# Normed x, context and rotated key: split in their own layout and turned by three DMA transposes per sequence instead of by TensorE

## The chip, the cores and the metric

The kernel runs on one core of a Trainium2 chip. The metric is the device time of one execution in microseconds (us). The core has a matrix engine (TensorE, PE in the profile, its weight loads PEld), VectorE (DVE), ScalarE (ACT), GpSimd (POOL) and SyncE (SP), whose instruction stream here does nothing but issue DMA transfers. Each engine works its own instruction list in order; they meet through semaphores (`wait_ge`, `then_inc`).

## What is computed

One transformer block over `x` (8 sequences of 128 tokens, width 256) and a context `ctx` of the same shape: layer norm, attention with 16 heads on 4 key/value groups over the 128 context tokens and 128 own tokens, output projection, residual; then a second layer norm, a shared feed-forward net and 8 experts of which each token takes 2.

```python
h = layernorm(x)
q, k, v = h @ wq, h @ wk, h @ wv                   # 16, 4, 4 heads of 128
q, k = rotate(rms_norm(q, qw)), rotate(rms_norm(k, kw))
k_ctx, v_ctx = rms_norm(ctx @ wk_ctx, kw), ctx @ wv_ctx
s = q @ concat(k_ctx, k).T / sqrt(128) + causal
x = x + (softmax(s) @ concat(v_ctx, v)) @ wo
x = x + moe(layernorm(x)) + shared(layernorm(x))
```

## The kernel before

Float32 values enter the matmuls as two fp16 parts, a high part (the rounded value) and a low part (value minus high part), and each product is three fp16 matmuls. ACT makes the high parts (L460, a helper `copy`), DVE most of the low parts (L908, a helper `low`); in the profile these lines stand for many tiles, so groups are told apart by the tile's name.

The attention part is a pipeline over the sequences b = 0 to 7 with four steps g = 0 to 3 each, one for each key/value group (4 heads). Each engine has a function `row(b, first, last)` with the same steps: written out for b = 0, as a loop for b = 1 to 6, written out for b = 7. In step g PE does: `scores(b, g)` (L1282, L1304), the turning of the rotated queries one step ahead (`q_turn`, L1261), the turning of the previous step's probabilities (`turn_probs`, L1315), the query projection two steps ahead (`q`, L1172), and `mix` of the previous step (probabilities times values, L1325). In between stand, in step 0, the value projections; in step 1, `out_proj(b - 1)`, 48 matmuls (L1352), and then `turn_inputs(b + 1)`; in step 2, after `q(b + 1, 0)`, the projections `kc(b + 1)` and `k(b + 1)` of context key and key; in step 3, `kc_turn` and `k_turn(b + 1)`. So the inputs and keys of sequence b + 1 are made within the row of b.

Three things are turned for each next sequence nb = b + 1 (contraction needs the width on the partitions):

- normed x: ACT makes `x_hi` and POOL `x_lo` in step 1, `turn_inputs` (L1197) turns both on PE into the PSUM bank `turn`, ACT's `in_copies` copies them to `xT`. Its first reader is `q(nb, 0)` in step 2.
- context: `ctx_b` is turned in float32 (L1200) into the same bank; ACT makes `cT_hi` from it, DVE `cT_lo` (`cT_low`, after `residual(b - 1)`, which waits for `out_proj`). First reader: `kc(nb)`.
- rotated key: POOL's `k_scale` (L758) writes `k_rot` in step 2, `k_turn` (L1229) turns it in step 3 into `proj[0]`, ACT's `k_copy` and DVE's `k_low` make `kT_hi` and `kT_lo`, both between other work of step 3. First reader: `scores(nb, 0)`.

ACT's step 3 runs `q_copy(nb, 0)`, `p_copy`, then `exps(b, 3)` (four exponentials, L549) with `kc_copy` and `k_copy` between the second and third. POOL ends step 2 with `k_roots`, `k_scale` and `q_roots(nb, 0)` and begins step 3 with `q_add(nb, 1)`. SP has little to do in the rows: one load of `ctx_b` each (L413, after `in_turned`) and, for the weights of the experts, three loads and six DMA transposes (L419, L424) between rows. After the attention it issues 16 DMA transposes (L447) of 128x1024 bf16 (256 KB), one for each expert and token half.

PE's clock has two levels; `keep_warm` in the opening runs matmuls for nothing to hold the upper one.

Of the kernel before, what the change touches and what calls it, by code (L numbers as in the profile page):

```python
# [5 lines left out]
ALU = mybir.AluOpType  # L6
# [38 lines left out]
def xattn_moe_kernel(nc, x, ctx, wq, wk, wv, wo, wk_ctx, wv_ctx, q_norm_w, k_norm_w,  # L45
# [14 lines left out]
    with ExitStack() as stack:  # L60
# [57 lines left out]
        x_hi = sb("x_hi", [P, D], FP16)  # L118
        x_lo = sb("x_lo", [P, D], FP16)
        xT = sb("xT", [P, 2, DC, P], FP16)  # L120
        cT = sb("cT", [P, DC, P])
        cT_hi = sb("cT_hi", [P, DC, P], FP16)
        cT_lo = sb("cT_lo", [P, DC, P], FP16)
# [27 lines left out]
        kT_hi = sb("kT_hi", [P, G, 2, P], FP16)  # L151
        kT_lo = sb("kT_lo", [P, G, 2, P], FP16)
# [101 lines left out]
        in_turned = sem("in_turned")  # L254
        xT_ready = sem("xT_ready")
        cT_high = sem("cT_high")
# [20 lines left out]
        k_high = sem("k_high")  # L277
        k_ready = sem("k_ready")
# [102 lines left out]
        def _(sp):  # L381
# [29 lines left out]
            def next_ctx(b):  # L411
                sp.wait_ge(in_turned, b)
                sp.dma_start(ctx_b[:], ctx[b, :, :]).then_inc(d_ctx, 16)  # L413

# [12 lines left out]
            next_ctx(2)  # L427
            next_ctx(3)
            sp.wait_ge(w1_cast, 4)
            sp.dma_start(w1_32[:], w3.rearrange("e h d -> h e d")).then_inc(d_w3, 16)  # L430
            turn_up(w1T, w1_b)
            next_ctx(4)
            sp.wait_ge(w3_cast, 4)
            sp.dma_start(w1_32[:].rearrange("p e (c h) -> p (e c) h", c=DC),
                         w2.rearrange("e (c p) h -> p (e c) h", p=P)).then_inc(d_w2, 16)
            turn_up(w3T, w3_b)
            next_ctx(5)
            sp.wait_ge(w2_cast, 4)
            turn_down()
            with sp.Fori(6, B) as b:  # L440
                next_ctx(b)
# [16 lines left out]
        def _(act):  # L458
# [10 lines left out]
            def ln_high(nb):  # L469
                act.wait_ge(ln_xs, nb + 1)  # L470
                seen(act, in_turned, nb)
                copy(x_hi[:], xs[:]).then_inc(ln_hi, 1)

            def in_copies(nb):
                act.wait_ge(in_turned, nb + 1)
                copy(xT[:].rearrange("p a c t -> p (a c t)"), turn[:, 0:256].bitcast(FP16)).then_inc(xT_ready, 1)
                if isinstance(nb, int) and nb == 0:
                    copy(flat(cT[:]), turn[:, 256:512], CW).then_inc(cT_ready, 1)
                else:
                    copy(flat(cT_hi[:]), turn[:, 256:512], C_SCALE).then_inc(cT_high, 1)  # L480
# [20 lines left out]
            def k_squares(nb):  # L501
                seen(act, k_mean, nb)
                squares(proj[1], k_ss, k_junk, k_t12, nb + 1, float(P) ** -0.5, k_sq)
# [22 lines left out]
            def k_copy(nb):  # L526
                act.wait_ge(k_turned, nb + 1)
                copy(kT_hi[:, :, 1, :], proj[0][:].rearrange("p (g t) -> p g t", g=G), K_SCALE).then_inc(k_high, 1)
# [74 lines left out]
            def row(b, first, last):  # L603
                for g in range(G):
# [7 lines left out]
                    exps(b, g, (kc_copy, k_copy) if g == 3 and not last else ())  # L612
# [8 lines left out]
                    if g == 1 and not last:  # L621
                        in_copies(b + 1)
# [12 lines left out]
                    if g == 0:  # L635
                        vc_copy(b)
                    if first and g == 1:
# [58 lines left out]
        def _(pool):  # L696
# [6 lines left out]
            nc.gpsimd.memset(eps_k[:], RMS_EPS * XW ** 2)  # L703
# [33 lines left out]
            def ln_low(nb):  # L737
                pool.wait_ge(ln_hi, nb + 1)
                seen(pool, in_turned, nb)
                nc.gpsimd.tensor_tensor(x_lo[:], xs[:], x_hi[:], ALU.subtract).then_inc(ln_lo, 1)  # L740
# [13 lines left out]
            def k_scale(nb):  # L754
                pool.wait_ge(k_added, nb + 1)
                pool.wait_ge(k_root, nb + 1)
                seen(pool, k_turned, nb)
# [117 lines left out]
        def _(dve):  # L875
# [35 lines left out]
            def cT_low(nb):  # L911
                dve.wait_ge(cT_high, nb)
# [660 lines left out]
```

## Time and profile before

| | us |
|---|---|
| median of 3 runs | 366.74 |
| lowest, highest | 364.2, 368.2 |
| profiled execution, its own time | 366.01 |
| its span | 364.3 |
| busy: PE, DVE, ACT, POOL | 329.9, 316.9, 263.7, 166.5 |

The profile is of one execution. Its span is 1.7 us shorter than that execution's own time. The prologue takes some 30 us, the eight rows run from there to about 310 us, the feed-forward part fills the rest. In the timeline each line gives start, duration, engine, line, operation, output<-inputs, shapes and count; in square brackets stands how long the engine was idle before it and what ended that. A duration of a PE matmul includes its way through the array, so the distance between two starts, not the duration, is what a matmul takes of PE.

### The profile page before, as it was taken

What the parts mean: (1) busy time and instruction counts of PE and PEld (TensorE: products, weight loads), DVE (VectorE), ACT (ScalarE), POOL (GpSimd) and SP (SyncE); (2) the same over time, 40 slices, a digit from 0 to 9 for tenths busy, and PEclk for the clock granted to TensorE, in tenths of its full rate; (3) what the DMA queues carried; (4) which work ended last, traced back from release to release, by engine and by line L of the source; (5) the groups of instructions that cost most, each with busy time, mean ns of one, the idle gap of its engine ahead of it and who ended that gap; (6) DMA issues with size and microseconds to landing.
All of it is one profiled execution on the core that took longest, in us unless ns stands there. A gap on an engine that the chain in (4) does not pass through costs nothing.

```text
span 364.3 us, 7426 instructions
## 1 busy us (share of the span) xinstructions
PE 329.9 (91%) x2296; PEld 223.4 (61%) x2296; DVE 316.9 (87%) x602; ACT 263.7 (72%) x916; POOL 166.5 (46%) x241
## 2 busy tenths in 40 slices
PE   6788698799999999999999999999999999987894
PEld 6365455376667666866576657565856687754351
DVE  1779999998999899989999998999899987967643
ACT  3668989576986798679768976897599748447341
POOL 4467656652755175427532734263426230362600
PEclk9899989999999999999999999999999999999999
DMA  6977000000042005200300000000000000167844
GB/s 177 380 238 230 18 0 2 1 2 14 1 126 47 14 0 128 45 14 3 58 6 8 0 0 14 0 0 0 0 0 0 3 0 0 23 123 75 159 75 129
DMA packets 34835, 19.25 MB, mean 53 GB/s; under 512 B 24056, under 2 KB 32256, under 8 KB 34816
## 3 DMA queue, kind: packets, MB, share of 16 engines
q1 hardware_dynamic: 34816, 19.02, 20.6%
q8 instruction: 9, 0.15, 0.2%
q14 instruction: 10, 0.08, 0.1%
HBM read 12.20 MB, written 1.05 MB: 36 GB/s over the span
## 4 chain that ended last, share of the span: by engine, by line
PE 35%; DVE 24%; ACT 18%; issue 10%; POOL 6%; DMA 3%; SPq 1%; DVEq 1%; ACTq 0%; POOLq 0%
PE proj L1352 10%; ACT probs L549 7%; DVE probs L982 5%; PE pt_ps L1315 5%; PE turn L1261 3%; DVE nmax L970 3%; POOL q_rot L772 3%; PE o_ps L1325 3%; DVE pT_lo L908 3%; PE proj L1172 3%; PE sc_ps L1282 3%; ACT pT_hi L460 2%; DVE q_t L899 2%; ACT kc_junk L493 2%; DMA wq<-in_L_xattn_wq_dram 2%
## 5 line engine op out<-in xcount | busy, mean ns | idle before, releaser
L549 ACT ACTIVATE probs<-sc_ps,nbias,q_r 128x256 f32<-128x256 f32 x128 | 70.8, 573 | 2.8 <-DVE nbias L974 2.8
L772 POOL TENSOR_TENSOR q_rot<-q_t 128x512 f32<-128x512 f32 x32 | 42.4, 1325 | 41.3 <-DVE q_t L901 40.5
L982 DVE TENSOR_SCALAR probs<-probs,rden 128x256 f32<-128x256 f32 x128 | 51.2, 461 | 1.1
L460 ACT ACTIVATE pT_hi<-pt_ps 128x512 f16<-128x512 f32 x64 | 34.8, 597 | 10.1 <-PE pt_ps L1315 10.1
L493 ACT ACTIVATE q_junk<-proj 128x128 bf16<-128x128 f32 x128 | 34.0, 294 | 10.8 <-DVE q_t L901 10.8
L1172 PE MATMUL proj<-wq_hi,xT 128*128 128x512 f16 x128 | 39.2, 389 | 2.1 <-DVE wq_lo L892 2.1
L908 DVE SCALAR_TENSOR_TENSOR pT_lo<-pt_ps,pT_hi 128x512 f16<-128x512 f32 x64 | 40.9, 680 | 0.1
L970 DVE TENSOR_REDUCE nmax<-sc_ps 128x4 f32<-128x1024 f32 x32 | 38.8, 1214 | 1.5 <-PE sc_ps L1304 1.5
L729 POOL TENSOR_TENSOR q_r<-q_me,power 128x4 f32<-128x4 f32 x32 | 33.4, 1044 | 2.5
L460 ACT ACTIVATE qT_hi<-turn 128x512 f16<-128x512 f32 x32 | 19.5, 610 | 20.5 <-PE turn L1261 20.5
L1315 PE MATMUL pt_ps<-ident,probs 128*128 128x128 f32 x256 | 34.1, 277 | 0.2
L1352 PE MATMUL proj<-wo_hi,oT_hi 128*128 128x256 f16 x112 | 30.5, 273 | 0.0
L1352 PE MATMUL proj<-wo_lo,oT_hi 128*128 128x256 f16 x112 | 30.5, 273 | 0.0
L1352 PE MATMUL proj<-wo_hi,oT_lo 128*128 128x256 f16 x112 | 30.5, 273 | 0.0
L1315 PEld LDWEIGHTS pt_ps<-ident,probs 128*128 128x128 f32 x256 | 29.4, 143 | 0.6 <-DVE probs L982 0.3
L1261 PE MATMUL turn<-ident,q_rot 128*128 128x128 f32 x128 | 19.8, 278 | 10.9 <-POOL q_rot L772 5.3
L493 ACT ACTIVATION_READ_ACCUMULATOR q_junk<-proj 128x1 f32 x128 | 28.5, 226 | 0.0
L549 ACT ACTIVATION_READ_ACCUMULATOR probs<-sc_ps,nbias,q_r 128x1 f32 x128 | 27.5, 215 | 0.0
L1325 PE MATMUL o_ps<-pT_hi,v_hi 128*128 128x512 f16 x64 | 24.3, 379 | 2.8 <-DVE pT_lo L908 2.8
L908 DVE SCALAR_TENSOR_TENSOR oT_lo<-o_ps,oT_hi 128x512 f16<-128x512 f32 x32 | 21.9, 685 | 5.4 <-ACT oT_hi L460 5.4
L460 ACT ACTIVATE oT_hi<-o_ps 128x512 f16<-128x512 f32 x32 | 19.6, 613 | 7.8 <-PE o_ps L1325 7.8
L1282 PE MATMUL sc_ps<-kT_hi,qT_hi 128*128 128x256 f16 x128 | 24.5, 273 | 0.5 <-ACT probs L549 0.2
(221 smaller groups left out, 882.8 us busy)
## 6 DMA issues: line engine op xcount, KB each, us to landing
wq<-in_L_xattn_wq_dram SPq DMA_DIRECT2D x4, 512.0 KB, 8.4
w<-in_L_ffn_w_dram SPq DMA_DIRECT2D x2, 1024.0 KB, 9.9
wq<-in_L_xattn_wo_dram SPq DMA_DIRECT2D x1, 2048.0 KB, 8.2
ctx_b<-in_ctx_dram SPq DMA_DIRECT2D x8, 128.0 KB, 2.0
out_dram<-x_all SPq DMA_DIRECT2D x4, 256.0 KB, 2.2
x_all<-in_x_dram SPq DMA_DIRECT2D x1, 896.0 KB, 12.0
wkc<-in_L_xattn_wk_ctx_dram SPq DMA_DIRECT2D x1, 512.0 KB, 3.9
wk<-in_L_xattn_wk_dram SPq DMA_DIRECT2D x1, 512.0 KB, 4.9
```

The lines of the kernel that those rows point to most:

```text
L460: return nc.scalar.activation(out_, in_, ACT.Copy, scale=scale)
L493: last = nc.scalar.activation(junk[:, head], bank[:, head], ACT.Square, scale=scale, accum_out=dst[:, h:h + 1])
L549: last = nc.scalar.activation(probs[:, h, :], sc_ps[:, h, :], ACT.Exp, bias=nbias[:, h:h + 1], scale=q_r[:, g, h:h + 1], accum_out=den[:, ...
L772: nc.gpsimd.tensor_tensor(q_rot[:], q_t1[:], q_t2[:], ALU.add).then_inc(q_added, 1)
L908: return nc.vector.scalar_tensor_tensor(out=lo, in0=src, scalar=scale, in1=hi, op0=ALU.mult, op1=ALU.subtract)
L970: nc.vector.tensor_reduce(nmax[:], sc_ps[:], AX_X, ALU.max, negate=True).then_inc(s_max, 1)
L982: last = nc.vector.tensor_scalar(probs[:, h, :], probs[:, h, :], rden[:, h:h + 1], None, ALU.mult)
L1172: last = nc.tensor.matmul(bank[:], xT[:, a, c, :], w[:, c, cols], start=(n == 0), stop=(n == 3 * DC - 1))
L1282: nc.tensor.matmul(sc_ps[:, h, :], a[:, h * P:(h + 1) * P], w[:, g, :, :].rearrange("p a t -> p (a t)"), start=start, stop=False, skip_gro ...
L1315: last = nc.tensor.transpose(pt_ps[:, a, h * P:(h + 1) * P], probs[:, h, a * P:(a + 1) * P], ident[:])
L1325: last = nc.tensor.matmul(o_ps[:], v[:, a, g * P:(g + 1) * P], p[:, a, :], start=(a == 0 and i == 0), stop=(a == 1 and i == 2))
L1352: last = nc.tensor.matmul(proj[0][:, 0:D], o[:, h // R, (h % R) * P:(h % R + 1) * P], w[:, h, :], start=(h == 0 and i == 0), stop=(h == H ...
```

## The change

TensorE no longer turns x, context and key for nb >= 1 (for nb = 0 all stays). Instead:

- Context: ACT's new `ctx_high` splits `ctx_b` as it lies, at the end of step 0 of the row before; DVE's `ctx_low` takes the place of `cT_low` in step 1. Both halves lie in the memory of `cT` (`c16`), and a DMA transpose writes `cT16`.
- x: `x_hi` and `x_lo` lie side by side (`x16`), and a DMA transpose writes `xT`.
- Key: ACT's `k_round` takes the rounding of `k_rot` ahead of `exps(b, 3)`, POOL's `k_rest` the low part at the head of its step 3, both into `k16` (the memory of `k_t1`), and a DMA transpose of 256 KB writes the halves of `kT`. `k_turn`, `k_copy` and `k_low` go for nb >= 1. The scale 2^4 moves into `eps_k` and the squares.
- SP issues them in a fixed order for each row: context, load of the next context, x, key; the weights' transfers come after the key of their row. The waits are in the diff. On PE, `q(nb, 0)` and `k(nb)` wait for `d_xT`, `kc(nb)` for `d_cT`, `scores(nb, 0)` for `d_kT`.

The core of the diff, in the order of the file: SP, then ACT (`ctx_high`, `k_round`), POOL (`k_rest`), DVE (`ctx_low`), and last PE (`k_turn` and `turn_inputs` go from its row).

```diff
+            for b in range(B - 1):
+                nb = b + 1
+                sp.wait_ge(c_high, nb)
+                sp.wait_ge(c_low16, nb)
+                sp.wait_ge(vc_proj, nb)
+                sp.dma_start_transpose(cT16[:].rearrange("p s c t -> p (s c) t"),
+                                       c16.rearrange("p s d -> p (s d)")).then_inc(d_cT, 16)
+                if nb + 1 < B:
+                    sp.dma_start(ctx_b[:], ctx[nb + 1, :, :]).then_inc(d_ctx, 16)
+                sp.wait_ge(ln_hi, nb + 1)
+                sp.wait_ge(ln_lo, nb + 1)
+                sp.wait_ge(q_proj, G * nb)
+                sp.wait_ge(v_proj, nb)
+                sp.dma_start_transpose(xT[:].rearrange("p s c t -> p (s c) t"),
+                                       x16[:].rearrange("p s d -> p (s d)")).then_inc(d_xT, 16)
+                sp.wait_ge(k_high16, nb)
+                sp.wait_ge(k_low16, nb)
+                sp.wait_ge(s_done, G * nb)
+                sp.dma_start_transpose(kT[:, :, :, 1, :].rearrange("p s g t -> p (s g) t"),
+                                       k16.rearrange("p s n -> p (s n)")).then_inc(d_kT, 16)
...
+            def ctx_high(nb):
+                act.wait_ge(d_ctx, 16 * (nb + 1))
+                act.wait_ge(vc_proj, nb)
+                seen(act, d_cT, 16 * (nb - 1))
+                copy(c16[:, 0], ctx_b[:], C_SCALE).then_inc(c_high, 1)
+            def k_round(nb):
+                act.wait_ge(k_norm, nb + 1)
+                copy(k16[:, 0], k_rot[:]).then_inc(k_high16, 1)
...
-                    exps(b, g, (kc_copy, k_copy) if g == 3 and not last else ())
+                    if g == 3 and not last:
+                        k_round(b + 1)
+                    exps(b, g, (kc_copy,) if g == 3 and not last else ())
...
-                    if g == 1 and not last:
-                        in_copies(b + 1)
...
+            def k_rest(nb):
+                pool.wait_ge(k_high16, nb)
+                nc.gpsimd.tensor_tensor(k16[:, 1], k_rot[:], k16[:, 0], ALU.subtract).then_inc(k_low16, 1)
...
+                    if g == 3 and not last:
+                        k_rest(b + 1)
...
+            def ctx_low(nb):
+                dve.wait_ge(c_high, nb)
+                low(c16[:, 1], ctx_b[:], C_SCALE, c16[:, 0]).then_inc(c_low16, 1)
...
-                        k_low(b + 1)
...
-                        cT_low(b + 1)
+                        ctx_low(b + 1)
...
-                        k_turn(b + 1)
...
-                        if not last:
-                            turn_inputs(b + 1)
```

The orders below are the compiled lists of instructions. First POOL, from the end of step 2 into step 3 of a row, before: `k_r` and `k_rot` are the key's factor and its scaling, `q_me` and `q_r` are `q_roots(nb, 0)`, `q_rot` is `q_add(nb, 1)`.

```order
L729 TENSOR_TENSOR k_r<-k_me,power 128x4 [waits k_mean]
L758 TENSOR_TENSOR k_rot<-k_sum,k_r 128x512 [waits k_turned,k_root,k_added]
L727 TENSOR_TENSOR q_me<-q_ss,eps_q 128x4 [waits q_sq,s_exp]
L729 TENSOR_TENSOR q_r<-q_me,power 128x4 [waits q_mean]
L772 TENSOR_TENSOR q_rot<-q_t 128x512 [waits q_turned,q_t12]
```

The same place of the changed kernel:

```order
L762 TENSOR_TENSOR k_r<-k_me,power 128x4 [waits k_mean]
L797 TENSOR_TENSOR k_rot<-k_sum,k_r 128x512 [waits k_high16,k_root,k_added]
L760 TENSOR_TENSOR q_me<-q_ss,eps_q 128x4 [waits q_sq,s_exp]
L762 TENSOR_TENSOR q_r<-q_me,power 128x4 [waits q_mean]
L803 TENSOR_TENSOR k_t<-k_rot,k_t 128x512 [waits k_high16]
L815 TENSOR_TENSOR q_rot<-q_t 128x512 [waits q_turned,q_t12]
```

The key's low part (L803) stands behind the two operations of `q_roots(nb, 0)` and ahead of `q_add(nb, 1)`. Next ACT in step 3 before: `p_copy` (pT_hi), then `exps(b, 3)` with the two key copies within.

```order
L460 ACTIVATE pT_hi<-pt_ps 128x512 [waits p_turned]
L460 ACTIVATE pT_hi<-pt_ps 128x512
L549 ACTIVATE probs,den<-sc_ps,nbias,q_r 128x256 [waits p_turned,s_bias]
L549 ACTIVATE probs,den<-sc_ps,nbias,q_r 128x256
L460 ACTIVATE kT_hi<-turn,kw_scaled 128x4x128 [waits kc_turned]
L460 ACTIVATE kT_hi<-proj 128x4x128 [waits k_turned]
L549 ACTIVATE probs,den<-sc_ps,nbias,q_r 128x256 x2
```

The same place of the changed kernel:

```order
L481 ACTIVATE pT_hi<-pt_ps 128x512 [waits p_turned]
L481 ACTIVATE pT_hi<-pt_ps 128x512
L481 ACTIVATE k_t<-k_rot 128x512 [waits k_norm]
L580 ACTIVATE probs,den<-sc_ps,nbias,q_r 128x256 [waits p_turned,s_bias]
L580 ACTIVATE probs,den<-sc_ps,nbias,q_r 128x256
L481 ACTIVATE kT<-turn,kw_scaled 128x4x128 [waits kc_turned]
L580 ACTIVATE probs,den<-sc_ps,nbias,q_r 128x256 x2
```

The copy out of `proj` within the exponentials is gone, and a rounding of `k_rot` (L481, into `k_t`) with a wait for `k_norm` stands ahead of all four. Last SP in two rows of the changed kernel (before there was one `ctx_b` load a row):

```order
L436 DMA_TRANSPOSE cT<-cT 128x4x128 [waits vc_proj,c_low16,c_high]
L439 DMA ctx_b<-in_ctx_dram 128x256
L444 DMA_TRANSPOSE xT<-x 128x4x128 [waits q_proj,v_proj,ln_lo,ln_hi]
L449 DMA_TRANSPOSE kT<-k_t 128x8x128 [waits s_done,k_low16,k_high16]
L453 DMA w_32<-in_L_ffn_w_dram 128x8x256 [waits w1_cast]
L423 DMA_TRANSPOSE w1T<-w_b 128x8x128 x2
```

The transpose of x stands behind the transpose of the context and behind the load of the next context.

## Rows read from the trace of the kernel before

**Rows 1.** The page: busy time of each engine, share of the span, count
```profile
PE 329.9 (91%) x2296; PEld 223.4 (61%) x2296; DVE 316.9 (87%) x602; ACT 263.7 (72%) x916; POOL 166.5 (46%) x241
```

**Rows 2.** Stretch, its length, busy PE, PEld, DVE, ACT, POOL, granted clock
```profile
189.80:225.30 35.50, 34.24 (x248) 23.75 (x246) 33.84 (x68) 28.32 (x108) 15.77 (x23) 1.00 0.01 4
```

**Rows 3.** Timeline from the end of out_proj to the next query projection
```profile
189.00 0.27 PE L1352 MATMUL proj<-wo_hi,oT_lo 128*128 128x256 f16 x1
189.11 0.28 PE L1197 MATMUL turn<-ident,x_hi 128*128 128x128 f16 x2
...
189.34 0.39 PE L1200 MATMUL turn<-ident,ctx_b 128*128 128x128 f32 x2
...
189.91 0.36 SPq L413 DMA_DIRECT2D ctx_b<-in_ctx_dram  x1
...
190.66 0.42 DVE L908 SCALAR_TENSOR_TENSOR cT_lo<-turn,cT_hi 128x256 f16<-128x256 f32 x1
```

**Rows 4.** Timeline of PE, step 2 and 3 of the same row
```profile
192.83 1.04 PE L1315 MATMUL pt_ps<-ident,probs 128*128 128x128 f32 x8
193.71 0.59 PE L1172 MATMUL proj<-wq_hi,xT 128*128 128x512 f16 x2
...
195.00 1.03 PE L1185 MATMUL turn<-wk,cT_hi 128*128 128x512 f16 x4
...
204.62 0.66 PE L1229 MATMUL proj<-ident,k_rot 128*128 128x128 f32 x4 [0.31 <-POOL k_rot L758]
206.40 0.38 PE L1282 MATMUL sc_ps<-kT_hi,qT_hi 128*128 128x256 f16 x2
...
216.76 0.63 PE L1261 MATMUL turn<-ident,q_rot 128*128 128x128 f32 x4 [0.41 <-DVE v_lo L908]
```

**Rows 5.** DMA issues: tile, kind, count, KB each, median us from issue to landing
```profile
ctx_b<-in_ctx_dram SPq DMA_DIRECT2D x8, 128.0 KB, 2.0
out_dram<-x_all SPq DMA_DIRECT2D x4, 256.0 KB, 2.2
w2T<-w_b SPq DMA_TRANSPOSE x2, 3.2
```

**Rows 6.** Timeline of SP's queue: two transposes of 256 KB each
```profile
175.08 2.61 SPq L424 DMA_TRANSPOSE w2T<-w_b  x2
```

**Rows 7.** Timeline of POOL and ACT around the key in step 3
```profile
203.52 1.04 POOL L758 TENSOR_TENSOR k_rot<-k_sum,k_r 128x512 f32<-128x512 f32 x1
...
204.79 1.01 POOL L729 TENSOR_TENSOR q_r<-q_me,power 128x4 f32<-128x4 f32 x1
...
203.58 0.57 ACT L549 ACTIVATE probs<-sc_ps,nbias,q_r 128x256 f32<-128x256 f32 x1
```

**Rows 8.** Timeline of ACT and POOL: the split of x
```profile
221.43 0.44 ACT L460 ACTIVATE x_hi<-xs 128x256 f16<-128x256 f32 x1
221.95 0.67 POOL L740 TENSOR_TENSOR x_lo<-xs,x_hi 128x256 f16<-128x256 f32 x1 [4.58 <-ACT x_hi L460]
```

**Rows 9.** Timeline of PE in the row of sequence 0 and after it
```profile
29.05 0.66 PE L1261 MATMUL turn<-ident,q_rot 128*128 128x128 f32 x4 [1.96 <-POOL q_rot L772]
...
45.28 1.85 PE L1315 MATMUL pt_ps<-ident,probs 128*128 128x128 f32 x8
46.91 1.06 PE L1172 MATMUL proj<-wq_hi,xT 128*128 128x512 f16 x2
...
49.12 1.03 PE L1185 MATMUL turn<-wk,cT_hi 128*128 128x512 f16 x4
...
60.82 0.38 PE L1282 MATMUL sc_ps<-kT_hi,qT_hi 128*128 128x256 f16 x2
...
69.78 0.39 PE L1325 MATMUL o_ps<-pT_hi,v_hi 128*128 128x512 f16 x1 [2.52 <-DVE pT_lo L908]
```

**Rows 10.** Busy time by stretch, as rows 2; the granted clock follows POOL
```profile
42.30:44.80 2.50, 0.00 (x0) 0.02 (x1) 2.50 (x7) 2.50 (x5) 2.42 (x3) 1.00 0.00 0
44.80:48.80 4.00, 3.99 (x17) 2.81 (x18) 3.97 (x5) 2.72 (x7) 2.99 (x1) 0.57 0.00 0
```

More of the change, by code:

```diff
@@ L277, in xattn_moe_kernel @@
         k_high = sem("k_high")
+        k_high16 = sem("k_high16")
+        k_low16 = sem("k_low16")
         k_ready = sem("k_ready")
@@ L470, in ln_high @@
                 act.wait_ge(ln_xs, nb + 1)
-                seen(act, in_turned, nb)
-                copy(x_hi[:], xs[:]).then_inc(ln_hi, 1)
+                if isinstance(nb, int) and nb == 1:
+                    act.wait_ge(in_turned, 1)
+                elif not isinstance(nb, int) or nb:
+                    act.wait_ge(d_xT, 16 * (nb - 1))
+                copy(x_hi, xs[:]).then_inc(ln_hi, 1)
             def in_copies(nb):
@@ L636, in row @@
                         vc_copy(b)
+                    if g == 0 and not last:
+                        ctx_high(b + 1)
                     if first and g == 1:
@@ L738, in ln_low @@
                 pool.wait_ge(ln_hi, nb + 1)
-                seen(pool, in_turned, nb)
-                nc.gpsimd.tensor_tensor(x_lo[:], xs[:], x_hi[:], ALU.subtract).then_inc(ln_lo, 1)
+                if isinstance(nb, int) and nb == 1:
+                    pool.wait_ge(in_turned, 1)
+                elif not isinstance(nb, int) or nb:
+                    pool.wait_ge(d_xT, 16 * (nb - 1))
+                nc.gpsimd.tensor_tensor(x_lo, xs[:], x_hi, ALU.subtract).then_inc(ln_lo, 1)
             def l2_root(b):
@@ L756, in k_scale @@
                 pool.wait_ge(k_root, nb + 1)
-                seen(pool, k_turned, nb)
+                if isinstance(nb, int) and nb == 1:
+                    pool.wait_ge(k_turned, 1)
+                elif not isinstance(nb, int) or nb:
+                    pool.wait_ge(k_high16, nb - 1)
                 nc.gpsimd.tensor_tensor(k_rot[:].rearrange("p (g d) -> p g d", g=G),
@@ L1204, in kc @@
             def kc(nb):
-                pe.wait_ge(cT_ready, nb + 1)
-                seen(pe, q_ready, G * nb)
-                if not (isinstance(nb, int) and nb == 0):
+                if isinstance(nb, int) and nb == 0:
+                    pe.wait_ge(cT_ready, 1)
+                else:
+                    pe.wait_ge(d_cT, 16 * nb)
+                    pe.wait_ge(q_ready, G * nb)
                     pe.wait_ge(wc_low, 1)
@@ L1239, in q @@
                 if g == 2:
-                    pe.wait_ge(k_ready, b + 1)
+                    if isinstance(b, int) and b == 0:
+                        pe.wait_ge(k_ready, 1)
+                    pe.wait_ge(q_sq, G * b + 1)
                 if g == 3:
@@ L1254, in q_turn @@
                     pe.wait_ge(v_ready, b + 1)
-                if g == 3 and last:
+                if g == 3:
                     pe.wait_ge(q_ready, G * b + g)
-                if g == 3 and not last:
-                    pe.wait_ge(xT_ready, b + 2)
-                    pe.wait_ge(cT_ready, b + 2)
                 for h in range(R):
@@ L1287, in scores @@
                 if g == 0:
-                    pe.wait_ge(k_high, b + 1)
+                    if isinstance(b, int) and b == 0:
+                        pe.wait_ge(k_high, 1)
+                    else:
+                        pe.wait_ge(d_kT, 16 * b)
                     pe.wait_ge(kc_high, b + 1)
@@ L1399, in _ @@
             keep_warm(32)
-            turn_inputs(0)
+            turn_inputs()
             keep_warm(16)
@@ L1412, in _ @@
             keep_warm(16)
-            k_turn(0)
+            k_turn()
             keep_warm(8)
```

95 lines of the change are left out of this document (48 added, 47 removed).

## Prediction

> **What bounds the kernel now.** I read the page first [rows 1]: PE is busy 91% of the span, VectorE 87%, so a reader might think that every matmul taken from PE pays. Then the busy time of one loop row [rows 2]: it takes 35.50 us and PE is busy 34.24 of it, VectorE 33.84. The eight rows are a chain in which PE runs from one operation to the next almost without a gap, and what decides is at which points PE would have to wait for something from outside. Two such points matter here: the first reader of the new x, `q(nb, 0)` at 193.71, and the first reader of the new key, `scores(nb, 0)` at 206.40 [rows 4]. The row shown is that of one b in the loop; all times below are in its clock.
>
> **What goes from PE.** `turn_inputs` begins right behind out_proj at 189.11, and its last two transposes start at 189.34 [rows 3]: with them some 0.45 us of PE. `k_turn` takes four transposes at 204.62 and 0.31 us of waiting ahead [rows 4], some 0.75 us. ACT loses three copies and gains two, VectorE loses one operation. All of this can only come back where nothing later is waited for.
>
> **Step A, x.** In the new order of SP the context is turned first. Its low part, `ctx_low`, stands on VectorE where `cT_low` stands now, behind the residual of out_proj: 190.66 + 0.42 = 191.08 [rows 3]; the shape is the same, so I keep that. SP started its load 0.18 us after the turning ended (189.34 + 0.39 = 189.73, start 189.91) [rows 3], so the context's transpose starts at 191.25. SP was held 2.61 us by two transposes of 256 KB [rows 6], 1.3 each; half of that for 128 KB, 0.65 (an estimate from that row), gives 191.9. The load of the next context holds SP 0.36 [rows 3], so the transpose of x starts at about 192.35. How long 128 KB take to land turned, no row shows. From below: a plain load of 128 KB lands in 2.0; from above: a transpose of 256 KB lands in 3.2 [rows 5]. I take 2.6, the middle, as half the data should save about half of what separates them. x lands at 194.95 and `q(nb, 0)` starts at 195.0 and not at 193.71: **1.3 us later** (0.7 to 1.9). PE, 0.45 early without `turn_inputs`, stands 1.75 us. The context, issued 1.1 us ahead, is there before `kc(nb)`, which stood at 195.00 and now comes at 196.3.
>
> **Step B, the key.** The projections, squares and factors that make `k_rot` follow `q(nb, 0)` in one chain, so `k_rot`, finished at 203.52 + 1.04 = 204.56 [rows 7], comes 1.3 later, at 205.85 (0.5 at least, since ACT's exponentials stand in that chain too). Then, new in line: ACT's `k_round`; `x_hi` took 0.44 for half the shape [rows 8], so 0.6 to 0.65: 206.5. It stands ahead of `exps(b, 3)`, which began at 203.58 [rows 7] and now begins at 206.5. `k_rest` on POOL can't start then, because the order shows the two operations of `q_roots(nb, 0)` between `k_rot` and it; they end at 204.79 + 1.01 = 205.80 now [rows 7], 1.24 behind `k_rot`, so 207.1. `k_rest` takes twice the 0.67 of `x_lo` [rows 8], 1.3: 208.4. SP 0.2: 208.6. A transpose of 256 KB lands in 3.2 [rows 5]: 211.8, and `scores(nb, 0)` starts at 211.9 instead of 206.40: **5.5 us later**, step A's 1.3 included. The last work ahead of it, `mix(b, 2)`, is over at about 207, so PE stands near 5 us. In that shadow lies the removed `k_turn`, which therefore returns nothing; the same holds for `turn_inputs` in that of step A. Nobody but PE waits for the key, but everything is behind PE: the next maximum, exponentials and probabilities all start from these scores. The exponentials of (b, 3), three microseconds late, end at about 209.3 and are thus covered; were the key there in time, they would be the next thing late.
>
> **What is caught up.** From `scores(nb, 0)` to the end of the next out_proj PE had one wait worth naming, 0.41 for `v_lo` [rows 4]. VectorE and ACT can use the stall to be ready, PE can't be faster: 0.4 us back. Leaves 5.1 us a row.
>
> **Step C, the clock.** In the row of sequence 0 PE stood idle from 42.30 to 44.80, and behind it the granted clock was 0.57 on average over 4 us, that is mostly the lower level of 1.2 GHz [rows 10]. The eight transposes of `turn_probs` then took 46.91 - 45.28 = 1.63 us and six projection matmuls 49.12 - 46.91 = 2.21 [rows 9]; the same in the loop row took 193.71 - 192.83 = 0.88 and 195.00 - 193.71 = 1.29 [rows 4]: 1.67 us lost for one fall. An idle of 1.96 us ahead of 29.05 left the matmuls behind it as they were (0.66 for the group against 0.63) [rows 9, 4]. So I expect the 5 us of step B to bring a fall and the 1.75 us of step A none. Part of the low stretch lies in the stall itself, so 1.5 us a fall. The Trainium skill, TensorE: Matmul & The Clock Gate, section "The HAM clock gate", has the same two levels and the drop after idleness; here the trace agrees, with the 2.5 us above.
>
> **Sum.** A loop row gets 5.1 + 1.5 = 6.6 us longer; six of them (b = 1 to 6): 39.6. The row of b = 0 prepares sequence 1 in the same way: its scores, at 60.82 [rows 9], come about 5.5 later, but PE waited 2.52 us at 69.78 for `pT_lo` [rows 9], which can take up as much; with the clock 5.5 - 2.5 + 1.5 = 4.5. The row of b = 7 prepares nothing: 0. The weights' transposes follow the key of their row, some 15 us ahead of the next context: 0. Together 44.1 on the profiled execution's 366.01, which is 0.7 below the median of the runs: **410 us**.
>
> A rule that speaks otherwise: the Trainium skill, Advanced Engine Details and Errata, section "X-Bar Transpose (TRN2)", says that transpose DMAs are as fast as regular ones. The rows differ for 256 KB: 3.2 turned, 2.2 plain [rows 5]. By the rule it would be rival 3 below.
>
> **The rivals.**
> 1. The clock stays up in the stalls of step B. For it: 1.96 us of idle did not lower it [rows 9]; against it: 2.5 us did [rows 10], and here it is 5. 366 + 6 x 5.1 + 3 = 400 us.
> 2. The stall of step A also lowers the clock, or the transposes land late (two more transfers share the queue): 1.5 a row more, 7 x 1.5 = 10.5: 421 us.
> 3. A turned transfer costs what a plain one does, 2.0 for 128 KB and 2.2 for 256 KB [rows 5]: 0.6 less in step A, 1.0 less in step B, seven times: 11 less, 399 us.
> 4. The other side: the transfers are hidden and PE gets its 0.45 and 0.75 us back each time: 7 x 1.2 = 8.4, 358 us. This decides itself where the key is turned within the time between `k_rot` at 204.56 and `scores(nb, 0)` at 206.40, 1.84 us; rounding, low part and transfer would have to fit, and the transfer alone takes 3.2.
>
> **Chances and range.** Forecast 0.60; rival 1 0.13; rival 2 0.15; rival 3 0.09; rival 4 0.01; a stall of step B nearly covered by something that I read wrongly, with less than 1% lost, 0.02. The range reaches from the bounds of rivals 1 and 3, less 0.8 a row if the key's chain moves by 0.5 only (399 - 6 = 393), to rival 2 with x landing at 3.2 (421 + 4 = 425). A measurement of this kernel tells about 1% from no change. Faster by over 1% 0.01, within 1% 0.02, slower 0.97.
>
> **What would show it.** In the changed kernel's waits: PE's `q` and `scores` lines wait for DMA `xT` and `kT`, seven times each, about 1.7 and 5 us. The loop row is 42 us long instead of 35.5. The granted clock falls to the lower level behind each wait for `kT`, not behind that for `xT`. The landing of `kT` is 3.2 and `xT` 2.6. POOL's L803 starts right behind `q_r`, and `probs` of step 3 starts behind `k_t<-k_rot`. Wrong would be: a row under 38 us, a key transfer issued before 207 of this clock, or a wait for something else at `scores`.

## The result, and the profile after

The changed kernel took 415.31 us (median of 4, 414.71 to 416.41), the kernel before 365.82 on the same chip (364.2 to 368.2): a ratio of 1.134, 95% interval 1.129 to 1.138. The forecast was 410, with a range of 393 to 425. The two profiled executions have spans of 414.0 and 364.3 us, 49.7 apart.

The page of the changed kernel: busy time by engine as in [rows 1], the granted clock in tenths by fortieths of the span, and two groups of matmuls (busy time, mean ns of one, idle time of PE ahead of them and what ended it).

```profile
PE 339.2 (82%) x2222; PEld 226.8 (55%) x2226; DVE 313.1 (76%) x595; ACT 260.6 (63%) x909; POOL 175.4 (42%) x248
...
PEclk9899897999899898999699989988999899999998
...
L1335 PE MATMUL sc_ps<-kT,qT_hi 128*128 128x256 f16 x256 | 56.3, 303 | 32.6 <-DMA kT<-k_t 32.6
...
L1218 PE MATMUL proj<-wq_hi,xT 128*128 128x512 f16 x128 | 40.0, 395 | 21.1 <-DMA xT<-x 18.7
```

The change takes ten transposes from PE in each of seven rows, 70 in all: its weight loads fall by just that, its matmuls by 74, as a few records of matmuls are missing. PE is nevertheless busy 9.3 us longer than in [rows 1], since more of its matmuls run at the lower clock. And it stands still for 32.6 us ahead of the scores and 18.7 us ahead of the projection of x, both times for a transposed transfer. Those two waits come to 51.3 us, beside 49.7 us of longer span. Not all of it is new: 5.0 us of the x wait stand in the row of sequence 0, ahead of 49.73, where the kernel before waited 2.56 us for VectorE's `cT_lo`. The x wait is 2.3 to 2.6 us in the loop rows of b = 1 to 5 and 1.63 in that of b = 6, which has no next context to load.

When the eight residuals on VectorE ran (first and last start; the first belongs to sequence 0, the last ends the row that prepares nothing), of before and then of after:

```profile
L992 DVE SCALAR_TENSOR_TENSOR x_all<-proj,x_all x8: 423/425/425, 82.8 to 317.8; 128x256 f32 x6, 128x256 f32<-128x256 f32 x2
```
```profile
L1039 DVE SCALAR_TENSOR_TENSOR x_all<-proj,x_all x8: 424/425/425, 88.2 to 367.5; 128x256 f32 x6, 128x256 f32<-128x256 f32 x2
```

By the first one the changed kernel is 5.4 us behind, and between the first and the last another (367.5 - 88.2) - (317.8 - 82.8) = 44.3 are lost: 7.4 in each of six loop rows. Behind the last nothing is lost or won: 367.5 - 317.8 is the whole 49.7.

One loop row of the changed kernel, x and context first (the timeline; what stands in brackets is idle time ahead and what ended it):

```profile
217.81 0.42 DVE L1039 SCALAR_TENSOR_TENSOR x_all<-proj,x_all 128x256 f32 x1 [0.23 <-PE proj L1409]
...
218.97 0.39 DVE L953 SCALAR_TENSOR_TENSOR cT<-ctx_b,cT 128x256 f16<-128x256 f32 x1
...
219.43 1.19 SPq L436 DMA_TRANSPOSE cT<-cT  x1
...
220.66 0.58 SPq L439 DMA_DIRECT2D ctx_b<-in_ctx_dram  x1
...
221.41 1.19 SPq L444 DMA_TRANSPOSE xT<-x  x1
...
224.19 0.59 PE L1218 MATMUL proj<-wq_hi,xT 128*128 128x512 f16 x2 [2.39 <-DMA xT<-x]
```

The low part of the context (`cT_lo` in [rows 3]) serves as the common mark. From it to `q(nb, 0)` it was 193.71 - 190.66 = 3.05 us in [rows 3, 4]; now it is 224.19 - 218.97 = 5.22, so x comes 2.2 us late. SP, the engine that issues the transfers, is occupied ("held" from here on) 1.19 us by the context's transpose and 0.58 by the next context's load before x gets its turn.

Then the key, in the same row and view:

```profile
233.83 1.04 POOL L797 TENSOR_TENSOR k_rot<-k_sum,k_r 128x512 f32<-128x512 f32 x1
...
234.91 0.63 ACT L481 ACTIVATE k_t<-k_rot 128x512 f16<-128x512 f32 x1 [1.00 <-POOL k_rot L797]
235.11 1.01 POOL L762 TENSOR_TENSOR q_r<-q_me,power 128x4 f32<-128x4 f32 x1
235.43 0.38 PE L1382 MATMUL o_ps<-pT_lo,v_hi 128*128 128x512 f16 x1
235.44 0.55 ACT L580 ACTIVATE probs<-sc_ps,nbias,q_r 128x256 f32<-128x256 f32 x1
...
236.09 1.15 POOL L803 TENSOR_TENSOR k_t<-k_rot,k_t 128x512 f16<-128x512 f32 x1
...
237.32 1.24 SPq L449 DMA_TRANSPOSE kT<-k_t  x1
...
240.62 0.58 PE L1335 MATMUL sc_ps<-kT,qT_hi 128*128 128x256 f16 x2 [4.80 <-DMA kT<-k_t]
```

`k_rot` is ready at 234.87; rounding, two small operations of POOL that are no part of the key (one of them L762), the low part and the transfer follow one after the other, and PE is idle from 235.81 on. From the mark to these scores it is 21.65 us, against 206.40 - 190.66 = 15.74 in [rows 3, 4]: 5.9 us late.

The clock around the two stalls (busy time by stretch, columns as in [rows 2], the granted clock ahead of the last two), first the key's stall in this row, then the x stall of the next:

```profile
239.00:240.00 1.00, 0.00 (x0) 0.00 (x0) 0.83 (x4) 0.82 (x4) 0.45 (x2) 1.00 0.87 162
240.00:241.00 1.00, 0.39 (x3) 0.29 (x4) 0.55 (x1) 0.00 (x0) 0.83 (x1) 0.72 0.00 0
241.00:242.00 1.00, 1.00 (x6) 0.73 (x5) 0.00 (x0) 0.00 (x0) 0.00 (x0) 0.50 0.00 0
...
243.00:244.00 1.00, 1.00 (x9) 0.87 (x7) 0.20 (x1) 0.00 (x0) 0.00 (x0) 0.57 0.00 0
...
268.00:269.00 1.00, 1.00 (x3) 0.30 (x2) 0.59 (x1) 0.00 (x0) 0.00 (x0) 0.50 0.00 0
...
270.00:271.00 1.00, 1.00 (x4) 0.32 (x3) 0.96 (x4) 0.00 (x0) 0.00 (x0) 0.50 0.00 0
```

The clock is at its lower level, 0.50 or 1.2 GHz, for some 3.4 us at the end of the key's stall and behind it (from 240.4 to 243.9). Behind the x stall in the row shown above it stayed at 1.00; in the next row, and in one other of the six, it fell as well. In all there are ten low stretches between 45 and 330 us, where the kernel before has one: seven at the key, three at x (the third is in the row of sequence 0, where the kernel before has its own). Two of the seven at the key, from 66.3 and from 196.0, are 6.8 us long.

### The profile page after: what moved, and what is told of

The parts are those of the page before. It is cut to its first block and busy times, and to the rows that moved or that the text cites. A ratio compares the mean times of both kernels' runs of the same rounds, so it can differ in the third digit from the quotient of the medians.

```text
span 414.0 us, 7308 instructions
## 1 busy us (share of the span) xinstructions
PE 339.2 (82%) x2222; PEld 226.8 (55%) x2226; DVE 313.1 (76%) x595; ACT 260.6 (63%) x909; POOL 175.4 (42%) x248
## 5 line engine op out<-in xcount | busy, mean ns | idle before, releaser
L1335 PE MATMUL sc_ps<-kT,qT_hi 128*128 128x256 f16 x256 | 56.3, 303 | 32.6 <-DMA kT<-k_t 32.6
L1218 PE MATMUL proj<-wq_hi,xT 128*128 128x512 f16 x128 | 40.0, 395 | 21.1 <-DMA xT<-x 18.7
L1335 PEld LDWEIGHTS sc_ps<-kT,qT_hi 128*128 128x128 f16 x256 | 26.7, 107 | 46.1 <-issue 35.8
L481 ACT ACTIVATE qT_hi<-turn 128x512 f16<-128x512 f32 x32 | 19.6, 611 | 44.6 <-PE turn L1314 44.6
L481 ACT ACTIVATE pT_hi<-pt_ps 128x512 f16<-128x512 f32 x64 | 34.8, 598 | 10.4 <-PE pt_ps L1372 9.8
L1372 PE MATMUL pt_ps<-ident,probs 128*128 128x128 f32 x256 | 35.0, 282 | 0.4 <-DVE probs L1029 0.3
L762 POOL TENSOR_TENSOR q_r<-q_me,power 128x4 f32<-128x4 f32 x32 | 33.5, 1046 | 2.5
L481 ACT ACTIVATE oT_hi<-o_ps 128x512 f16<-128x512 f32 x32 | 19.4, 607 | 22.9 <-PE o_ps L1382 22.9
L1372 PEld LDWEIGHTS pt_ps<-ident,probs 128*128 128x128 f32 x256 | 30.6, 147 | 0.9 <-DVE probs L1029 0.9
L944 DVE TENSOR_TENSOR q_t<-proj,q_cos 128x512 f32<-128x512 f32 x32 | 21.8, 683 | 11.6 <-PE proj L1218 11.6
L1218 PEld LDWEIGHTS proj<-wq_hi,xT 128*128 128x128 f16 x128 | 12.4, 101 | 31.6 <-issue 16.0
L1335 PE MATMUL sc_ps<-kT,qT_lo 128*128 128x256 f16 x128 | 28.0, 305 | 0.1
```

The lines of the kernel that those rows point to most:

```text
L481: return nc.scalar.activation(out_, in_, ACT.Copy, scale=scale)
L762: nc.gpsimd.tensor_tensor(r, me, power[:], ALU.pow).then_inc(root, 1)
L1218: last = nc.tensor.matmul(bank[:], xT[:, a, c, :], w[:, c, cols], start=(n == 0), stop=(n == 3 * DC - 1))
L1335: nc.tensor.matmul(sc_ps[:, h, :], a[:, h * P:(h + 1) * P], w[:, g, :, :].rearrange("p a t -> p (a t)"), start=start, stop=False, skip_gro ...
L1372: last = nc.tensor.transpose(pt_ps[:, a, h * P:(h + 1) * P], probs[:, h, a * P:(a + 1) * P], ident[:])
```

## The experiments

Each was timed beside the kernel before, which had medians of 366.95, 367.04 and 366.92 us in the three groups that ran together; the changed kernel's own 415.31 is compared by ratio.

**1. x ahead of the context on SP.** The rest of the changed kernel stays.

```diff
+                sp.wait_ge(ln_hi, nb + 1)
...
+                sp.dma_start_transpose(xT[:].rearrange("p s c t -> p (s c) t"),
+                                       x16[:].rearrange("p s d -> p (s d)")).then_inc(d_xT, 16)
                 sp.wait_ge(c_high, nb)
...
                     sp.dma_start(ctx_b[:], ctx[nb + 1, :, :]).then_inc(d_ctx, 16)
-                sp.wait_ge(ln_hi, nb + 1)
...
-                sp.dma_start_transpose(xT[:].rearrange("p s c t -> p (s c) t"),
-                                       x16[:].rearrange("p s d -> p (s d)")).then_inc(d_xT, 16)
```

> The changed kernel with one edit: SP issues the transpose of x ahead of that of the context and of the context load. Its waits are the same; x is split some 4 us before the context's low part is there. Theory (x is late only because it stands in SP's queue behind the context, and the whole chain from the query projection to the rotated key follows it): PE's wait for xT (2.4 to 2.7 us a row in the changed kernel) goes to zero, the key's transpose is issued about 2 us earlier in the row, so a row gets 2.1 us shorter plus the occasional fall of the clock behind the wait for x: 415 - 7 x 2.5 = about 398 us. Rival (the late x only fills time that the key's transfer would leave idle anyway): PE's wait for kT grows by what that for xT loses, the time stays at 413 to 415.

Measured: 399.16 us, ratio 1.089 (1.084 to 1.095), 16 us less than the changed kernel from the order of two entries alone. The waits of PE between 85 and 330 us (sum, times, longest):

```profile
PE sc_ps L1335 <- DMA kT<-k_t: 27.7, 6, 4.7
PE turn L1314 <- POOL q_rot L815: 3.3, 6, 0.5
```

The wait for x is gone and that for the key has kept its length. So the stall ahead of `q(nb, 0)` came from SP's order. The transfer itself takes 2.4 us to land instead of 2.5, but it now starts while PE still has other work. The clock's part is mixed into these 16 us: no low stretch is left at x, while those at the key are now 6.8 us long in six of the seven rows, with 4.7 to 5.5 us of each behind the stall's end.

**2 and 3. The key turned by PE again,** once with the order of the change (2) and once with x first (3). `k_turn` on PE, `k_copy` on ACT and `k_low` on VectorE are back as in the kernel before.

```diff
-                sp.dma_start_transpose(kT[:, :, :, 1, :].rearrange("p s g t -> p (s g) t"),
-                                       k16.rearrange("p s n -> p (s n)")).then_inc(d_kT, 16)
...
-                    if g == 3 and not last:
-                        k_round(b + 1)
-                    exps(b, g, (kc_copy,) if g == 3 and not last else ())
+                    exps(b, g, (kc_copy, k_copy) if g == 3 and not last else ())
...
-                        k_rest(b + 1)
...
+                        k_turn(b + 1)
```

> The changed kernel with the key turned by TensorE again for every sequence (k_turn, k_copy, k_low as before; k_round, k_rest and the key's DMA transpose gone), x and context still by DMA in the changed kernel's order. Theory (two separate costs, some 2.1 us a row from x and some 5.5 from key and clock): the row is 35.5 + 2.1 - 0.4 = 37 to 38 us, and the clock falls in some rows behind the wait for x: 366 + 7 x 2 + up to 4 = 380 to 384 us. Rival (nearly all of the cost hangs on the key): 366 to 370 us, with the wait for xT absorbed by later slack.

> Both edits together: key by TensorE as before, x and context by DMA with x issued first. Nothing waits for a transfer any more if the theory holds: x lands during the output projection, the context (issued at 191.25 of the row shown of the kernel before, landing in 2.5) at 193.8, ahead of its reader at 194.5. What is left is the pure gain of turn_inputs leaving TensorE: 0.45 us in each of 7 rows, 366 - 3 = 363 us. Rival (the row is set by VectorE and ACT as much as by PE, so that 0.45 us of PE are worth nothing): 366 us. Second rival (the context becomes the late one): a wait for cT at kc of 0.3 to 1 us a row, 366 to 370 us.

Measured: 383.61 us, ratio 1.047 (1.041 to 1.053), and 366.41 us, ratio 0.998 (0.996 to 1.001). In (2) PE's wait for x is what it was (13.4 us in six rows). In (3) no wait for a DMA is left in the loop rows, which are 35.1 us long (x's transposes start at 190.84 and 225.93), 0.4 less than in [rows 2]: that is all of the removed PE work that ever comes back. It isn't seen in the total, because the row of sequence 0 loses about as much; experiment 4 shows how much. The timeline of (3) there:

```profile
46.77 1.20 SPq L442 DMA_TRANSPOSE cT<-cT  x1
...
47.08 0.59 PE L1201 MATMUL proj<-wq_hi,xT 128*128 128x512 f16 x2
...
50.10 0.68 DVE L937 SCALAR_TENSOR_TENSOR qT_lo<-turn,qT_hi 128x512 f16<-128x512 f32 x1
50.88 2.72 PE L1214 MATMUL turn<-wk,cT 128*128 128x512 f16 x6 [3.21 <-issue]
```

PE stands 3.2 us ahead of `kc`, the first reader of the context, and the granted clock is 0.50 behind it. At first sight the context is late, and the expectation of experiment 4 takes it so. But the context's transposes land at most 2.5 us after their issue in this trace, this one by 49.3. `kc` also waits for VectorE's `qT_lo` (`q_ready`), and that ends at 50.78, 0.1 us ahead of PE's start. The profile names no releaser; by these times it is `qT_lo`.

**4. The low part of the context earlier in (3),** so that its transpose doesn't wait.

```diff
                     if g == 3 and not last:
                         kc_low(b + 1)
...
+                    if g == 1 and not last:
+                        ctx_low(b + 1)
...
-                    if g == 1 and not last:
-                        ctx_low(b + 1)
```

(The two places are in VectorE's program; the first is its earlier one within a step.)

> Key by TensorE as before, x and context by DMA with x issued first, and VectorE's low part of the context moved from behind the residual to ahead of the normalisation of the same step, 3 to 4 us earlier. Without that move the loop rows took 35.1 us instead of 35.5, but in the row of sequence 0 TensorE waited for the context and the clock fell behind it, and the time was that of the kernel before. Theory (with the context early too, no transfer is waited for anywhere and 0.4 us a row stay): 366.9 - 7 x 0.4 = 364 us, no wait for cT. Rival (the move only makes VectorE's probabilities 0.4 us later in each row and gives the gain back): 367 us.

Measured: 365.85 us, ratio 0.996 (0.993 to 0.999), between the theory's 364 and the rival's 367. The context's first transpose now starts at 41.06 instead of 46.77 and has landed by 43.6, and yet:

```profile
47.59 0.68 DVE L937 SCALAR_TENSOR_TENSOR qT_lo<-turn,qT_hi 128x512 f16<-128x512 f32 x1
...
48.37 2.72 PE L1214 MATMUL turn<-wk,cT 128*128 128x512 f16 x6 [2.87 <-issue]
...
71.19 0.39 PE L1359 MATMUL o_ps<-pT_hi,v_hi 128*128 128x512 f16 x1 [3.50 <-DVE pT_lo L937]
```

PE still stands 2.87 us ahead of `kc`, again up to 0.1 us behind the end of `qT_lo`. So the wait in this row is VectorE's, not the transfer's. The residuals of this kernel, first and last start:

```profile
L1021 DVE SCALAR_TENSOR_TENSOR x_all<-proj,x_all x8: 409/425/425, 85.3 to 317.8; 128x256 f32 x6, 128x256 f32<-128x256 f32 x2
```

Before it was 82.8 and 317.8. The six loop rows gain 2.5 us, 0.4 each, and the row of sequence 0 loses the same 2.5. Its second stall, for `pT_lo`, is 3.50 us where it was 2.52 [rows 9], and the clock falls behind it, where it stayed up before. This is the only version whose interval lies below the kernel before, and by under half a per cent: x and context by DMA gain next to nothing even when neither is waited for.

**5. The key alone turned by DMA,** x and context by PE as in the kernel before.

```diff
+                sp.dma_start_transpose(kT[:, :, :, 1, :].rearrange("p s g t -> p (s g) t"),
+                                       k16.rearrange("p s n -> p (s n)")).then_inc(d_kT, 16)
...
+                    if g == 3 and not last:
+                        k_round(b + 1)
...
+                        k_rest(b + 1)
...
-                        k_turn(b + 1)
```

> Only the key is turned by DMA; x and the context are turned by PE as in the kernel before. Theory (the two stalls add up): the key's chain starts 2.1 us earlier than in the changed kernel, so scores are about 3.7 us late instead of 5.8, and the clock still falls behind them in every row (1.6). 3.7 + 1.6 - 0.4 of catching up = 4.9 in each of six loop rows, about 3 in the row of sequence 0: 366 + 32 = 398; it should also be what is left of 415.3 when the 17.6 us of x and context (the run with the key on PE, 383.6 against 366) are taken off. Rival (the x stall costs nothing of its own once the key stall is there, because the key transfer is what everything waits for): 408 to 415. Loop rows about 40.4 us, PE's wait at the scores about 3.5 us.

Measured: 400.44 us, ratio 1.091 (1.084 to 1.098): near the first theory's 398 and well below the rival's 408. The key alone costs 9.1%, x and context alone (2) 4.7%: together 13.8%, beside 13.4% for the whole change. In the total the two stalls add. The row in this kernel:

```profile
142.29 1.23 SPq L438 DMA_TRANSPOSE kT<-k_t  x1
...
145.81 0.61 PE L1310 MATMUL sc_ps<-kT,qT_hi 128*128 128x256 f16 x2 [4.92 <-DMA kT<-k_t]
```

PE stands 4.6 to 4.9 us in the six loop rows here too, not the 3.5 that I had expected. The load of the next context, at 125.03 in this row and at 189.91 in [rows 3], is the common mark: the scores come 20.78 us behind it instead of 16.49, so 4.3 late. I had taken them for 3.7 late; the removed `k_turn` lies in the shadow besides.

**6. Idle matmuls that keep the clock up.** The changed kernel, with matmuls whose result nobody reads ahead of the two waits: 24 ahead of x and 56 ahead of the key.

```diff
+            def hold_clock(count):
+                for _ in range(count):
+                    nc.tensor.matmul(proj[0][:, 0:P], identb[:], causal[:], start=True, stop=True)
...
-                    normed(b)
...
+                    if not isinstance(b, int) or b:
+                        hold_clock(24)
+                    normed(b)
...
+                        pe.wait_ge(q_sq, G * b + 1)
+                        pe.wait_ge(q_t12, G * b + 1)
+                        hold_clock(56)
                         pe.wait_ge(d_kT, 16 * b)
```

> The changed kernel with TensorE kept busy in its two stalls by matmuls whose result nobody reads: 24 of 128 columns ahead of the wait for xT, 56 ahead of the wait for kT (about 0.06 us each, 1.4 and 3.4 us, both less than the waits). They change nothing but the clock. Theory (each fall to 1.2 GHz costs some 1.6 us, 7 falls behind kT and some 3 behind xT): the granted clock stays at 1.00 in the rows and the time falls by 7 x 1.6 + 3 x 1.7 = 16 to about 399 us, with waits for the transfers as long as before. Rival (the low clock only slows matmuls that other engines would make wait anyway): clock at 1.00 and still 412 to 415 us.

(The wait for x, `normed(b)`, is also moved behind two other waits, so that it comes last.) Measured: 398.51 us, ratio 1.088 (1.082 to 1.094), the 399 of the theory. The clock line of its page:

```profile
PEclk9899989999999999999999999999999999999998
```

Behind the sixth fortieth of the span the clock stays up all through the rows. The transfers are as late as before: from the first query projection to the scores it is 16.41 us in a row of this kernel (214.87 to 231.28) and 16.43 in the row shown of the changed one (224.19 to 240.62). So the 16.8 us less than 415.31 are the price of the clock alone, and the 398.51 - 366.95 = 31.6 us that remain are that of lateness.

**7. The same, ahead of x only.**

```diff
-                    normed(b)
...
+                    if not isinstance(b, int) or b:
+                        hold_clock(24)
+                    normed(b)
```

> As the changed kernel, with 24 additional matmuls of 128x128 ahead of PE's wait for x, whose result nobody reads; none ahead of the wait for the key. They keep PE busy in the x stall. Theory (the clock also falls behind the x stall, in the row of sequence 0 and in two of six loop rows as the changed kernel's trace shows, 1.6 us each): 415.3 - 5 = 410. Rival (no fall behind x costs anything, since each is hidden by the key stall later in the row): 414 to 416. The granted clock stays at 1.00 behind every wait for x and is at 0.50 behind every wait for the key.

Measured: 411.7 us, ratio 1.121 (1.114 to 1.128), between the two theories' 410 and 414 to 416; its interval ends 0.001 below where that of the changed kernel begins. By this the clock behind x would cost about 4 us of the 16.8. Behind the x stall of the six loop rows it stayed up, as meant; in the row of sequence 0, where PE still stood 3.63 us, it fell. I don't take this one number for more: in this execution two of four low stretches at the key between 120 and 320 us were 6 to 7 us long, in the changed kernel's one of four, so that part of what x gave back may have been lost again there.

**8. The key in two transfers of 128 KB,** the high half as soon as ACT has rounded it.

```diff
-                sp.wait_ge(k_high16, nb)
-                sp.wait_ge(k_low16, nb)
-                sp.dma_start_transpose(kT[:, :, :, 1, :].rearrange("p s g t -> p (s g) t"),
-                                       k16.rearrange("p s n -> p (s n)")).then_inc(d_kT, 16)
+                sp.wait_ge(k_high16, nb)
+                sp.dma_start_transpose(kT[:, 0, :, 1, :], k16[:, 0]).then_inc(d_kT, 16)
+                sp.wait_ge(k_low16, nb)
+                sp.dma_start_transpose(kT[:, 1, :, 1, :], k16[:, 1]).then_inc(d_kTl, 16)
```

> The changed kernel with the key's transpose of 256 KB cut into two of 128 KB: the high part is sent as soon as ACT has rounded it, the low part when GpSimd has it; TensorE waits for the high part ahead of the scores and for the low part only ahead of the last third of them. Theory (the wait for kT is a chain of rounding, low part and transfer, and 128 KB land in 2.5 us where 256 KB take 3.1): the high part is issued at 235.7 instead of 237.3 in the row shown of the changed kernel and lands at 238.2, the low part at 239.8, so the scores begin 2.3 us earlier and wait once more for about 0.6 us inside: 1.7 us a row, 415 - 12 = 403 us, and less if the shorter idleness spares some falls of the clock. Rival (two transposes close behind each other land together, since each holds SP 1.2 us whatever its size): under 0.7 us a row, 410 us or more.

Measured: 399.56 us, ratio 1.090 (1.084 to 1.095). The timeline of one row:

```profile
230.21 1.20 SPq L449 DMA_TRANSPOSE kT<-k_t  x1
...
231.91 1.20 SPq L451 DMA_TRANSPOSE kT<-k_t  x1
...
232.90 0.38 PE L1337 MATMUL sc_ps<-kT,qT_hi 128*128 128x256 f16 x2 [2.44 <-DMA kT<-k_t]
...
234.40 0.28 PE L1337 MATMUL sc_ps<-kT,qT_hi 128*128 128x256 f16 x1 [0.47 <-DMA kT<-k_t]
```

Eight of the twelve products in these scores need only the high half. PE's first wait falls from 4.8 to 2.4 us, and the second is 0.47. That it came out 3 us better than forecast has a reason in the same rows: two of these matmuls take 0.38 us, as in [rows 4], where in the changed kernel they take 0.58 to 0.63. In this row the shorter stall did not lower the clock, and it did so at only three of the seven keys (at all seven in the changed kernel).

**9. POOL's `k_rest` ahead of `q_roots`.**

```diff
                         k_scale(b + 1)
-                        q_roots(b + 1, 0)
...
                         k_rest(b + 1)
+                        q_roots(b + 1, 0)
```

> The changed kernel with GpSimd's two operations for the factor of the next queries (q_roots of the next sequence's group 0) moved behind the key's low part. Theory: the low part starts right behind ACT's rounding, at 235.6 instead of 236.09 in the row shown, the key's transpose and the scores behind it follow 0.5 us earlier, 7 rows: 3.5 us, 411.5 us. Rival (nothing moves, because the wait is set elsewhere, or the factor itself becomes late for the first maximum): 415 us or more.

Measured: 411.31 us, ratio 1.119 (1.115 to 1.123), as the theory has it (411.5): 4 us less, and 0.5 in each wait for the key (25.9 us in six rows instead of 28.7).

**10. Everything together that shortens the DMA version:** x first, the key in halves, POOL's order, and 24 idle matmuls ahead of the key.

> All that shortens the key's path by DMA in one kernel: x issued first, the key in two halves, the low part ahead of the query factor, and 24 idle matmuls (1.4 us) ahead of the wait for the key to hold the clock. Theory (the costs are separate and add): 399 of x first, less 7 x 1.7 for the halves, less 7 x 0.5 for the order, less 7 x 1.6 for the clock: 373 us, with a rest of 1 to 1.5 us a row for which the scores still come later than in the kernel before; so the key by DMA stays slower than by TensorE even so. Rival (the key's transfer is fully hidden once it is cut): 364 to 367 us. Second rival (the parts overlap and do not add): 380 us or more.

Measured: 373.09 us, ratio 1.016 (1.011 to 1.020). PE still waits for the key seven times, 5.6 us in all. So the gap of 49.5 us shrinks to 6 with all three transposes still on the DMA queue. Its loop rows are 36.3 us long (between two turnings of the rotated queries, 206.71 and 243.04), 0.8 more than in [rows 2], and a wait for the key of 0.9 us is left in each of five of them: what these four edits do not take out of the key's chain.

## Why the prediction came out as it did

The forecast of 410 is 5 us under the 415.3 measured. All its mechanisms were found: the same two waits, in the same places, seven times each, none of the removed PE work given back, and the clock behind the key. Two terms were too small: what holds SP ahead of x, and how often and for how long the clock is low.

**Step A, x: too small.** I had x 1.3 us late; it was 2.2. The failing term is "half of that for 128 KB, 0.65". SP was held 1.19 by 128 KB, 1.24 by 256 KB. A hold was taken to shrink with the data, and it doesn't. The next load held SP 0.58, not 0.36. Together 0.54 + 0.22 = 0.8 of the 0.9 missing. The landing, where I had chosen the middle of two bounds, was right: the DMA issues of the changed kernel (size where given, median us to landing) have

```profile
ctx_b<-in_ctx_dram SPq DMA_DIRECT2D x8, 128.0 KB, 2.3
cT<-cT SPq DMA_TRANSPOSE x7, 2.5
xT<-x SPq DMA_TRANSPOSE x7, 2.5
kT<-k_t SPq DMA_TRANSPOSE x7, 3.1
```

2.5 against the 2.6 assumed, 3.1 against 3.2. PE stood 2.4 us, not 1.75. In the row of sequence 0, for which no x stall was worked out, it stood 5.0.

**Step B, the key: right.** 5.5 us late was expected, 5.9 found. Step A's 2.2 had become 2.0 by the end of `k_rot` (13.90 us behind the mark before, 15.90 now), 0.7 more than assumed; `k_rest` took 1.15 instead of 1.3, and SP started 0.08 behind it instead of 0.2. The links stand as they were written down: `probs` behind `k_t` (235.44 behind 234.91), `q_r` between `k_rot` and L803, a wait of 4.8. (9) shows what that small piece of POOL's order is worth, (5) that the chain costs 9% by itself.

**Step C, the clock: right at the key, wrong behind x, and its reason doesn't hold.** At every wait for the key it fell. I had excluded a fall behind the x stall, because 1.75 us is less than the 1.96 that left it up in [rows 9], while 2.5 lowered it in [rows 10]. Behind the real stalls it fell in two of six loop rows (2.45 and 2.63 us; not with 2.28, 2.32, 2.39 and 1.63). But the length of a stall decides nothing at this size. In [rows 9] themselves a stall of 2.52 us, ahead of 69.78, left the clock up (the matmul takes 0.39 us). And behind the very same stall of 1.96 us the clock fell in six of the twelve traces; here the one of (3):

```profile
29.46 1.02 PE L1295 MATMUL turn<-ident,q_rot 128*128 128x128 f32 x4 [1.96 <-POOL q_rot L801]
```

The group takes 1.02 us, where it takes 0.66 in [rows 9], and the clock is at 0.50 from 29.6 to 33.1. And the stall of 2.56 us in the row of sequence 0 that lowered the clock in the kernel before left it at 1.00 in the kernel with the key alone by DMA (5). So the line that I drew between 1.96 and 2.5 us isn't there: that no fall was forecast behind x was a guess, and that most rows agreed with it was partly luck.

With 1.5 us a fall the forecast counted 7 x 1.5 = 10.5 us for the clock; (6) measured 16.8. The price of one stretch was about right and their number was not. (6) took away nine low stretches of the changed kernel, seven at the key and two at x, and two of the nine were twice as long: eleven times 3.4 us, which makes 16.8 / 11 = 1.5 us for each. This is an estimate, since the count is from one execution and the 16.8 from medians.

**The sum.** A loop row was to be 6.6 longer and was 7.4: 0.4 from the later scores, and about as much from falls behind x and the long low stretch. Six rows: 4.7 of the 5.6 us missing in the spans. The row of sequence 0 with what stands ahead of it was to be 4.5 longer and was 5.4. It came there in another way than forecast: PE stood 5.0 us for x and 3.84 for the key, not 5, the low stretch at the key was 6.8 us long, and the wait for `pT_lo` of 2.52 was gone, as assumed.

**The rivals.** Rival 1, the clock stays up: not so; but made so in (6), 398.5 beside the 400 worked out for it. Rival 2, the x stall lowers the clock too: true in two of the six loop rows. Rival 3, a transposed transfer costs what a plain one does: 2.5 against 2.0 to 2.3, and 3.1 against 2.2 [rows 5]: the transposed one is slower at both sizes, and more so at 256 KB. Rival 4, hidden: not as changed. (3) and (4) show that x and context can be hidden if x goes first, and that this brings 0.4 us a loop row, which the row of sequence 0 takes back. For the key none of the orders tried hides it.

## What to carry to other kernels

A transfer that replaces work of a busy engine pays only where its result isn't the next thing that this engine needs: count the whole chain from the last producer to the first reader (rounding, both halves, the queue, the landing), and set it against the time that the old way left between those two points. Here that was 1.8 us (`k_rot` ready at 204.56, scores at 206.40 [rows 7, 4]), and the new chain took 5.75 (234.87 to 240.62). Look at what stands ahead of it on its queue: the order of two entries was worth 16 us of 49. And where a stall of a few microseconds recurs, add the clock behind it: here it was a third of the loss. For stalls of 2 to 2.6 us give both outcomes a chance instead of drawing a line between two lengths. Last, when a wait has no named releaser, set the landing of the transfer beside the end of every other thing that the instruction waits for, before the transfer is blamed.

## What the runs showed of the hardware

A small transpose is no cheaper to issue than a larger one. SP was held 1.19 us for 128 KB and 1.24 for 256 KB, and two of 128 KB cost it twice 1.20. A plain load of 128 KB held it 0.33 us in the kernel with only the key by DMA and 0.58 where it stood right behind a transpose; the one load of the changed kernel that began 0.45 us behind the transpose ahead of it (at 263.32) was held 0.33 again.

Stalls of one length had different outcomes. Behind the stall of 1.96 us ahead of the rotated queries in the opening, the same in all kernels, the clock fell in six of the twelve traces and stayed up in six. Behind x in (9), 2.31 us lowered it in one row and 2.32 did not in the next; 2.41 to 2.44 us ahead of the key's high half in (8) lowered it in two rows and not in three others. Every stall of 3.5 us and more in these traces, without idle matmuls in it, did.

The low stretches were 3.4 or 6.8 us long. At the key they were 3.4 us in five of seven rows of the changed kernel, and 6.8 in five of seven with the key alone by DMA (5) and in six of seven with x first (1). The long ones began 1.2 to 2.8 us before PE's stall ended, the short ones within 0.5 us of its end. What decides between the two was not tried.
